# The last of four chunks forms 24 of its pair steps in row form, and the top layers run as seven short visits

## What is computed

```python
e = stack([tbl_f[ids[:, f]] for f in range(40)], axis=1)      # 2048 x 40 x 64, float32
i_idx, j_idx = triu_indices(40, k=1)                          # 780 pairs
viW = einsum('bpd,pde->bpe', e[:, i_idx], W)                  # W: 780 x 64 x 64
z = einsum('bpe,bpe->bp', viW, e[:, j_idx])                   # 2048 x 780
h = concatenate([z, dense_ctx], axis=1)                       # 2048 x 796
h = maximum(h @ W_top1 + b_top1, 0)                           # 512 wide
h = maximum(h @ W_top2 + b_top2, 0)                           # 256 wide
y = h @ W_top3                                                # 2048 x 1
```

## Time and profile before

| | us |
|---|---|
| median of 3 runs | 1567.65 |
| profiled execution, whole | 1575.01 |
| profiled execution, span of its instructions | 1572.3 |
| first chunk's products | 41.7 to 513 |
| second, third chunk's products | 513 to 891, 891 to 1240 |
| last chunk, its steps 0 to 41 | 1240 to 1334 |
| last chunk, its steps 42 to 84 | 1334 to 1410 |
| last chunk, its steps 85 to 195 | 1410 to 1537 |
| top layers of the last chunk | 1537 to 1572 |

### The profile page before, as it was taken

One profiled execution on the slowest core, in us unless ns is written; L12 is line 12 of the kernel. 1 busy time (PEld: TensorE's weight loads), 2 busy tenths in 40 slices (PEclk: granted clock), 3 DMA queues, 4 the chain that ended last, 5 costly groups with the idle time before them and its releaser, 6 DMA issues.

```text
span 1572.3 us, 52519 instructions
## 1 busy us (share of the span) xinstructions
PE 1453.6 (92%) x21300; PEld 651.2 (41%) x21300; DVE 972.5 (62%) x841; ACT 870.1 (55%) x6611; POOL 741.2 (47%) x891
## 2 busy tenths in 40 slices
PE   4788989879889999989999999999999999999999
PEld 2344645535455433333333443333443443333333
DVE  2554545536555545566777665677777655679990
ACT  0544344436546644456867573455767643458992
POOL 6434434454444433436666564446676644553220
PEclk7788999989999999999999999999999999999999
DMA  4232223223222112222222222222222212222200
GB/s 124 64 106 68 77 63 80 70 57 84 72 76 73 49 48 52 76 60 51 58 60 65 50 52 59 70 70 59 57 60 59 57 54 59 73 60 60 57 9 14
DMA packets 60957, 98.79 MB, mean 63 GB/s; under 512 B 17062, under 2 KB 17078, under 8 KB 60715
## 3 DMA queue, kind: packets, MB, share of 16 engines
q1 hardware_dynamic: 35876, 65.08, 14.2%
q0 software_dynamic: 20224, 20.75, 7.1%
q10 hardware_dynamic: 4614, 9.61, 1.9%
HBM read 95.37 MB, written 0.01 MB: 61 GB/s over the span
## 4 chain that ended last, share of the span: by engine, by line
PE 88%; issue 6%; another core or an unknown queue 3%; DVE 3%; ACTq 0%; ACT 0%; DVEq 0%
PE u L1182 37%; PE u L1168 22%; PE zacc L1196 18%; PE u L1238 5%; PE u L1111 2%; DVE prod L1066 2%; PE u L1255 2%; PE u L1226 1%; PE u L1214 0%; DVE row_prod L1035 0%; DVE row_prod_v L1035 0%; DVE row_sums L1076 0%; ACTq L754 0%; ACT L880 0%
## 5 line engine op out<-in xcount | busy, mean ns | idle before, releaser
L926 ACT ACTIVATE row_prod<-row_prod 128x64 f32<-128x64 f32 x3248 | 777.0, 241 | 191.4 <-DVE row_prod L1035 146.6
L1066 DVE TENSOR_TENSOR prod<-u,emb 128x1024 f32<-128x1024 f32 x496 | 593.3, 1218 | 348.3 <-remote 151.0
L1182 PE MATMUL u<-emb,weights 64*32 64x512 f32 (+1 forms) x9760 | 753.0, 520 | 50.4 <-issue 32.7
L812 POOL DMA_INDIRECT gathered<-tbl,index x512 | 487.3, 952 | 568.5 <-DVE prod L1066 240.5
L926 ACT ACTIVATION_READ_ACCUMULATOR row_prod<-row_prod 128x1 f32 x3248 | 609.7, 188 | 3.9 <-issue 3.9
L1168 PE MATMUL u<-row_weights,emb 64*32 64x512 f32 (+5 forms) x5632 | 467.0, 534 | 22.3 <-issue 15.1
L1182 PEld LDWEIGHTS u<-emb,weights 64*32 64x32 f32 x9760 | 277.9, 108 | 382.6 <-issue 268.6
L1196 PE MATMUL zacc<-prod,band 64*32 64x512 f32 (+1 forms) x4960 | 403.9, 515 | 16.9 <-issue 12.4
L1035 DVE TENSOR_TENSOR row_prod<-u,first_fields 128x1024 f32<-128x1024 f32 x203 | 247.1, 1217 | 138.9 <-PE u L1168 83.3
L1168 PEld LDWEIGHTS u<-row_weights,emb 64*32 64x32 f32 x5632 | 150.6, 108 | 218.7 <-issue 137.7
L1196 PEld LDWEIGHTS zacc<-prod,band 64*32 64x32 f32 x4960 | 159.0, 109 | 167.2 <-issue 153.0
(11 more groups left out here) (41 smaller groups left out, 228.1 us busy)
## 6 DMA issues: line engine op xcount, KB each, us to landing
weights<-w_pairs SPq DMA_DIRECT2D x155, 256.0 KB
row_weights<-w_rows SPq DMA_DIRECT2D x90, 256.0 KB
gathered<-tbl,index POOLq DMA_INDIRECT x512
w12s<-w_top ACTq DMA_DIRECT2D x8, 832.0 KB
w12s<-w_top ACTq DMA_DIRECT2D x4, 512.0 KB
first_fields<-tbl,index POOLq DMA_INDIRECT x120
h<-tbl SPq DMA_DIRECT2D x2, 224.0 KB
h<-tbl ACTq DMA_DIRECT2D x2, 224.0 KB
```

The source lines that it names most:

```text
L812: pool.indirect_dma_start(out=to, out_offset=None, in_=tables[2 * t + e], in_offset=bass.IndirectOffsetOnAxis(ap=index[:, col:col + 1].bit ...
L926: last = nc.scalar.activation(x, x, ACT.Copy, accum_out=row_sums[:, c % 2, s, q:q + 1])
L1066: nc.vector.tensor_tensor(result, products, x, ALU.mult).then_inc(prod_ready, 1)
L1182: last = nc.tensor.matmul(u[of, b, h, to], weights[half, x % WRING, unit, of], y, start=True, stop=True)
```

## The change

- The last chunk alone (`KIND` 1) has 100 column steps and 96 row steps, still 196 together. Its new row steps (`XS`, six pieces of four steps) form pairs with fields 8 to 11, which stay batch-major in one buffer `more_fields` of tiles 4 and 5. A new piece joins the rows of two tiles, so each tile of the array gets two matmuls of 256 columns (32 instructions a step). The last chunk's weights, order and top weights are its own.
- `POOL_EVERY` becomes (4, 4, 4, 2), `VECTOR_RING` 3, `LEVEL_SPACE` 8. Rows by engine (ScalarE, VectorE, GpSimd) go from 54, 8, 10 to 43, 21, 8 in the second chunk, from 48, 8, 16 to 39, 21, 12 in the third, and from 48, 8, 16 to 38, 21, 37 in the last.
- The top layers are seven visits of one result block: four of layer 1, two of layer 2, one of layer 3. In the last chunk they stand at steps 42, 62, 82, 101, 120, 139 and 158. For chunks of kind 0 a block of layer 1 is made in two halves of 256 samples, in two banks; the last 64 rows of it for both halves run in the two row halves of the array at once. For the last chunk a block is seven matmuls of 512 columns. The weights of a visit are 448 KB (832 KB before), of layer 2 256 KB (512 KB).
- The dense inputs of the last chunk go straight into free rows of `z` by one DMA, in place of the transposed row sums.

```diff
+KEPT = 6
+MORE = range(2 * FT, 2 * KEPT)
+KIND = (0, 0, 0, 1)
-VECTOR_RING = 2
+VECTOR_RING = 3
-POOL_EVERY = 4
+POOL_EVERY = (4, 4, 4, 2)
-LEVEL_SPACE = 10
+LEVEL_SPACE = 8
...
-TOP_GROUPS = M1 // 2 + M2 // 2 + 1
+TOP_GROUPS = M1 + M2 + 1
...
-        new = [("col", k, t) for k in range(HUB + 1, t)]
+        new = [("col", k, t) for k in range(hub + 1, t) if kind == 0 or t < 2 * FT or k not in (KEPT, KEPT + 1)]
...
+for j, x in enumerate(XS):
+    a, b = 2 * FT + 2 * j, 2 * FT + 2 * j + 1
+    RUNS[x] = tuple(((2 * a + h, 0, len(MORE)), (2 * b + h, len(MORE), FF)) for h in (0, 1))
+    AGAINST[x] = [*MORE, *MORE]
...
+def make_row_steps(kind):
+    tiles = [1, 0]
+    for t in range(FT, T):
+        tiles.append(t)
+        if kind and t > 2 * FT and t % 2:
+            tiles.append(XS[(t - 2 * FT) // 2])
+    return [("row", t, s) for t in tiles for s in range(SUB)]
...
-    others = [x for x in rows if x >= POOL_FROM and x not in on_vector]
-    on_pool = set(others[POOL_EVERY - 1::POOL_EVERY])
+    on_pool = set()
+    for c, every in enumerate(POOL_EVERY):
+        others = [x for x in rows if x >= POOL_FROM and x // N == c and x not in on_vector]
+        on_pool.update(others[every - 1::every])
...
+                    if t in XS or t == 1:
+                        x = more_fields[:, s:s + 1, :] if t in XS else first_fields[:, c % 2, s:s + 1, 0:FT * DIM]
+                        x = x.broadcast_to([P, 4, FT * DIM])
...
+                        if KIND[c]:
+                            last = nc.tensor.matmul(u[:, b, 0, :], w12s[:, x % 2, q, :], z_blocks(c, q)[:, 0, :],
+                                                    start=(q == 0), stop=(q == ZG - 1))
+                            continue
+                        for h in (0, 1):
+                            half = slice(h * DIM, (h + 1) * DIM) if q == ZG - 1 else slice(0, P)
+                            at = slice(h * CB // 2, (h + 1) * CB // 2)
+                            last = nc.tensor.matmul(u[:, b, h, 0:CB // 2], w12s[half, x % 2, q, :],
+                                                    z_blocks(c, q)[half, 0, at], start=(q == 0), stop=(q == ZG - 1))
```

356 lines of the change are left out of this document (182 added, 174 removed).

## The result

The changed kernel takes 1577.63 us, median of 19 runs (1570.54 to 1585.48), the kernel before 1571.27 in 19 runs of the same comparison: a ratio of 1.0033, interval 1.0018 to 1.0049, or +5.2 us (the medians are 6.4 us apart). The forecast was +17. The sign held, the size did not: about a third of it came.

A forecast was written before the change was run, and what follows sets the result against it. TensorE and VectorE were taken as level and full after the gathers, with slower steps while gathers run. Terms -1 - 4.6 + 5 + 16 + 1.5 gave +17 us on 1567.65, so 1585 us, range 1562 to 1604.

The forecast's parts named there:

- Part 1: Last chunk: 24 column steps become row steps, saving TensorE 10.3 us, of which 2 us was taken as gain.
- part 4: Last chunk, steps 42 to 84: visits +3.4, ring stopping VectorE +3, share of Part 1 -1; together +5 us.
- Part 2: Second and third chunk: seven shorter visits cost +11 us, fewer slow steps give -12; together -1 us.
- rival (c): Visits: half-width matmuls are paced by weight loads, not columns, giving 1616 us; chance 0.07.
- Part 3: Last chunk, steps 0 to 41: 89 us against 93.8, so -4.6 us, with the interlock included.
- Part 5: Last chunk, steps 85 to 195: VectorE's 12 reductions and the visits cost +16 us, with a floor of 13.6.
- Part 6: The end: 56 layer 1 instructions take 24.1 us against 22.5, so +1.5 us.
- Rival (a): Steps 0 to 41: GpSimd keeps up, interlock costs little since TensorE is late; 12 us less, 1573; chance 0.16.
- the interlock: Last chunk: VectorE's product waits for GpSimd's earlier row, whose additions stand behind gathers awaiting later products; 8.2 us per four steps.
- Rival (d): A granted clock of 0.8 in Part 3; chance 0.10.

The follow-up runs named there:

- the visits alone: Kernel before with only the seven visits changed, the last chunk's at steps 21 to 139, old rows and shares: 1.0034 of the kernel before (quick), 0.9989 (held).
- the kernel with early visits: Kernel before with the seven visits, the last chunk's at steps 21 to 82, none behind step 85: 0.9887, 0.9925 and 0.9952 of the kernel before, held groups.

## Why the prediction was wrong

- **What bounds the kernel.** Right for the late stage: TensorE and VectorE level and full, to 0.1 us in every group. Wrong in one reading: "while gathers run it is slower" was taken as a property of the kernel, and the slow step at 1312.61 as the doing of a dense run of gathers. They come with gathers by index, in groups that suffer from them: 351.4 us in a held trace for the 196 steps that took 270.4 with plain DMAs in a held one, and 270.0 with gathers in a quick one.
- **Part 1.** Nothing gained behind the gathers, as said; that the halves cost nothing was nearly right (12 of 20 new row steps at 0.86 us, 8 at 1.07). Of the 2 us taken here only the 1 in part 4 entered the sum. What was not priced is that the 24 rows need an engine: 15 us in the quick group with ScalarE summing them, with the moved layer 1 visit in it.
- **Part 2.** -1 forecast, +2.5 measured. The visit was put at 6.6 us and is 6.0; its half-width matmuls, each with a weight load of its own, start every 0.22 us and not every 0.43, so rival (c) is out. The 12 us for fewer slow steps did not come: the held stretches of the two chunks went from some 49 to 43. The +11 did not come either: the quick traces have no slow steps to save, and there the two chunks changed by -0.9 us (+1.3 with the visits alone, where 6 were expected). That the sum of the two was near is luck.
- **Part 3.** This is the step that failed: -4.6 forecast, -10.1 measured. The mechanism is there as described, with its product, its ring and the gathers between, but its term was mis-sized: it runs over 6 periods and not 8 (the rows before the visit at step 42 are VectorE's, so no row of GpSimd follows that of step 34), and a period is 7.8 us, not 8.2. Steps 10 to 34 took 46.6 us for 49.2, and 34 to 42 with the visit 16.5 for 21.3; steps 0 to 10 took 20.5 for 18.5.
- **Part 4.** +5 forecast, +2.2 measured. The visits and the ring's stops are there (in the quick traces the stage grows by 13.3, 72.1 for 58.8), but 17 of the 75.8 us of before are held time, which the quick trace does not have, and in the held trace the stage grows by 2.2 alone. The wait and the slow pace were added, where they lie over each other.
- **Part 5.** +16 forecast, +15.8 measured, and half for a wrong reason: the forecast put it on VectorE's 12 reductions and called 13.6 us the floor. Taking them away gave 2.4. TensorE's visits cost the same beside them: the late stage of the kernel with early visits, which has no visits, no reductions and no new rows there, is 126.7 us again. The number came out near by luck.
- **Part 6.** +1.5 forecast, +1.3 measured.
- **The first chunk** gave 3.9 of the missing us, and it is chance: nothing in it changed, and its products took 459.7 to 472.6 us in the held traces.

The step that failed is part 3, and part 4 with it: a wait was priced as if it came on top of a pace whose cause was not known. Of the 9 us between forecast and trace, parts 3 and 4 hold 8.3 and the first chunk 3.9, less the 3.5 that the second and third chunk took more. Rival (a), "the interlock of part 3 costs little, because TensorE is late anyhow", gave +5 at a chance of 0.16, and +5 was measured. That is in part luck. It asked for steps 0 to 41 in 77 us and they took 83.7, for the interlock did set their pace; and 3.9 us came from the first chunk. What is right in it is the sum over steps 0 to 84: taking the interlock out in a held group gained nothing there. What spoke against it, 1.83 us of GpSimd's work a step, was true (39.6 of 46.6 us in 24 steps is 1.65), but TensorE's held time fills much of the same time. In a quick group the forecast would have been wrong the other way, with +29. Rival (d), at a chance of 0.10, was a granted clock of 0.8 in part 3, and no run shows it: the granted clock was 0.96 in steps 0 to 41 and 0.98 in 42 to 84, where 1.00 stood before, and 46.6 to 46.7 us passed in the interlocked steps at 0.93 as at 0.96.

## What to carry to other kernels

A stage with idle time of unknown cause can't carry a sum: price a new wait there twice, once as if the idle time stayed and once as if the wait filled it, and let both be ends. Moving work behind the point where two engines become level cost its whole length here: three visits of 7.9 us of TensorE's time, with six reductions, cost 9.5 there, and moved back ahead of it they cost 3.9. A step that spares one engine a sum gives the sum to another: count who does it before counting the saving.

## What the runs showed of the hardware

In three of the five groups, and in the comparison of the result, TensorE issued its instructions slowly in places while GpSimd issued gathers by index: mostly one to three weight loads, then the next about 0.75 us later (median in the first trace of the kernel before), nothing waited for. The kernel before took 1547 to 1571 us with it and 1138 without. Plain DMAs of 128 rows in the same places did not do it in the one run that had them (270.4 us for 351.4), and they occupied GpSimd for 0.55 us each in place of 0.95:

```profile
L813 POOL DMA_DIRECT2D gathered<-tbl x127 | 69.5, 548 | 100.9 <-DVE prod L1069 46.5 <-DVE row_prod L1038 42.0 <-DVE row_prod_p L1038 7.7
```

The first product of a trace tells the two sorts apart: it starts at 41.5 to 42.0 us in the held traces and at 20.7 to 21.3 in the quick ones. With two exceptions the runs of a group were alike, so a comparison within a group is sound; one between a held and a quick group is not, and one between two groups of a sort is good to some us.
